# Summing one quad of batches in six float32r passes instead of two float32 products

## The reference

```
h = relu(layernorm(x))
h = relu(adj @ (h @ Wg0 + bg0)); h = relu(adj @ (h @ Wg1 + bg1))     # per batch
for p in 1..4:          # windows of p nodes, an LSTM of p steps over each window
    last = lstm(h[:, windows of p nodes])
    h[:, last node of each window] = last
x = x + h
h = relu(layernorm(x))
V0, V1, V2 = h @ W[0], h @ W[1], h @ W[2]
out = x + diag(adj)*V0 + triu(adj,1) @ V1 + tril(adj,-1) @ V2 + bias
```

## Time and profile before

| what | value |
|---|---|
| median of 3 runs | 393.39 us (393.28 to 394.52) |
| the profiled execution's own time | 394.06 us |
| its span, first to last instruction | 391.6 us |
| PE busy | 386.2 us (99%), 2346 matmuls |
| PEld busy | 341.1 us (87%) |
| DVE busy | 334.4 us (85%), 867 instructions |
| ACT busy | 279.9 us (71%), 556 instructions |
| POOL busy | 64.2 us (16%) |
| TensorE clock granted | 1.000 of full speed, on average over the span |

### The profile page before, as it was taken

The page is one execution under the profiler, slowest core; times in us unless marked ns, Lnnn a source line. Parts: engine busy times, 40 slices in busy tenths (PEclk is TensorE's granted clock), DMA queues, the critical chain, the costliest instruction groups (busy, mean ns, idle before and its releaser), DMA issues.

```text
span 391.6 us, 6502 instructions
## 1 busy us (share of the span) xinstructions
PE 386.2 (99%) x2346; PEld 341.1 (87%) x2346; DVE 334.4 (85%) x867; ACT 279.9 (71%) x556; POOL 64.2 (16%) x67
## 2 busy tenths in 40 slices
PE   8999999999999999999999999999999999999996
PEld 8787899997976889899777889899897788989986
DVE  6669999998988788897998888989798958778895
ACT  4768776876597786777389777777659868667563
POOL 4820200101440003001043000300134000000242
PEclk9999999999999999999999999999999999999999
DMA  6940000005282000122366000030529200000045
GB/s 203 381 191 3 0 0 2 1 2 107 39 140 68 0 28 0 38 98 54 56 109 136 27 2 28 2 134 2 110 27 190 53 0 28 0 28 1 4 77 163
DMA packets 12559, 24.76 MB, mean 63 GB/s; under 512 B 4720, under 2 KB 6000, under 8 KB 11632
## 3 DMA queue, kind: packets, MB, share of 16 engines
q0 software_dynamic: 3600, 10.49, 15.1%
q1 hardware_dynamic: 8928, 13.87, 10.2%
HBM read 16.99 MB, written 4.22 MB: 54 GB/s over the span
## 4 chain that ended last, share of the span: by engine, by line
PE 59%; DVE 5%; DMA 1%; issue 1%; ACT 1%; POOL 1%; DVEq 0%; POOLq 0%
PE PS L612 9%; PE PS L613 9%; PE PS L628 8%; PE PS L659 5%; PE PS L648 5%; PE PS L649 5%; PE PS L708 4%; PE PS L552 2%; PE PS L529 2%; PE PS L562 2%; PE PS L700 2%; PE PS L544 2%; PE PS L701 2%; PE PS L702 2%; DMA X<-bias_row 1%
## 5 line engine op out<-in xcount | busy, mean ns | idle before, releaser
L975 ACT ACTIVATE GT<-PS,BG 128x256 f32<-128x256 f32 (+2 forms) x312 | 158.4, 564 | 16.0 <-PE PS L659 12.5
L612 PE MATMUL PS<-HH,WIH 128*128 128x256 f32 (+2 forms) x312 | 106.2, 341 | 0.3 <-DVE X L1241 0.3
L613 PE MATMUL PS<-HH,WIL 128*128 128x256 f32 (+2 forms) x312 | 102.7, 330 | 0.0
L628 PE MATMUL PS<-HL,WIH 128*128 128x256 f32 (+2 forms) x287 | 94.5, 329 | 0.0
L990 ACT ACTIVATE TC<-CS 128x512 f32<-128x512 f32 (+2 forms) x88 | 44.9, 510 | 45.9 <-DVE CS L1121 33.8
L612 PEld LDWEIGHTS PS<-HH,WIH 128*128 128x128 f32 x312 | 58.7, 188 | 10.0 <-DVE HH L1162 4.2
L430 POOL TENSOR_TENSOR RS<-VE,NHALF 128x4 f32<-128x4 f32 (+2 forms) x18 | 34.0, 1888 | 202.5 <-DVE VE L1057 131.4
L613 PEld LDWEIGHTS PS<-HH,WIL 128*128 128x128 f32 x312 | 58.8, 188 | 4.1 <-issue 1.2
L648 PE MATMUL PS<-SH,WHH 128*128 128x256 f32 (+2 forms) x192 | 59.9, 313 | 0.0
L649 PE MATMUL PS<-SH,WHL 128*128 128x256 f32 (+2 forms) x192 | 59.6, 311 | 0.0
L659 PE MATMUL PS<-SL,WHH 128*128 128x256 f32 (+2 forms) x189 | 59.0, 312 | 0.0
(11 more groups left out here) (107 smaller groups left out, 646.6 us busy)
## 6 DMA issues: line engine op xcount, KB each, us to landing
out_tbd<-X SPq DMA_DIRECT2D x15, 256.0 KB, 2.0
X<-x_tbd SPq DMA_DIRECT2D x3, 1024.0 KB, 11.8
H<-x_dbt SPq DMA_DIRECT2D x3, 1024.0 KB, 5.7
H<-HF POOLq DMA_DIRECT2D x6, 512.0 KB, 4.7
X<-bias_row POOLq DMA_DIRECT2D x6, 512.0 KB, 6.9
H<-means POOLq DMA_DIRECT2D x6, 256.0 KB, 5.1
H<-means POOLq DMA_DIRECT2D x3, 512.0 KB, 5.7
WI<-wih_t SPq DMA_DIRECT2D x1, 1024.0 KB, 5.6
```

Of the source, the lines that this page charges most:

```text
L612: pe.matmul(dst, WIH[:, p - 1, cols], x_high, start=True, stop=False)
L613: pe.matmul(dst, WIL[:, p - 1, cols], x_high, start=False, stop=False)
L628: mm = pe.matmul(dst, WIH[:, p - 1, cols], x_low, start=False, stop=(j == 0))
L975: act.activation(GT[:, s, q, 0:n], bank(s, q)[:, 0:n], ACT.Tanh if q == C else ACT.Sigmoid, bias=BG[:, 4 * (p - 1) + q:4 * (p - 1) + q + 1 ...
```

## The change

Quad 2 of groups 0, 1 and 2 (`PARTED = (2,)`) is summed in another way. ACT rounds V1 and V2 of the quad to float32r in two halves of two batches (256 columns for each side, 512 elements a partition) and puts them into a new tile; this stands in units 10 and 12, between the gates and the tanh. DVE subtracts, also in two halves, and puts the rest into the same tile; this is a `late` piece of units 10 and 12. PE sums the quad in six float32r passes of 512 columns: high parts of adj by high values and low parts of adj by high values for each side, then high parts of adj by low values for each side. The parts of adj's sides (256 columns) are made once, in body 0: the high part by ACT behind unit 18, the low part by DVE behind unit 19.

```
+PARTED = (2,)
+PART = "part"
+HIGH_PART_AT = {10: (2, 0), 12: (2, 1)}
-START_LATE = {4: ((OWN, 0),), 5: ((LOW, 2),), 9: ((LOW, 3),)}
+START_LATE = {4: ((OWN, 0),), 5: ((LOW, 2),), 9: ((LOW, 3),), 10: ((PART, (2, 0)),), 12: ((PART, (2, 1)),)}
-LATE_HIGH_AT = {6: ("wi",), 7: ("wh",), 16: ("wl",)}
-LATE_LOW_AT = {7: ("wi",), 9: ("wh",), 18: ("wl",)}
+LATE_HIGH_AT = {6: ("wi",), 7: ("wh",), 16: ("wl",), 18: ("adj",)}
+LATE_LOW_AT = {7: ("wi",), 9: ("wh",), 18: ("wl",), 19: ("adj",)}
...
+            def parted_sum(g, q, ps):                                   # PE
+                high, low = parts_of(0), parts_of(1)
+                pe.wait_ge(part_high, parted_before(g, q, 1) + 1)
+                for k in range(SIDES):
+                    pe.matmul(ps[:, :], ADJH[:, k, :], high[:, k, :], start=(k == 0), stop=False)
+                    pe.matmul(ps[:, :], ADJL[:, k, :], high[:, k, :], start=False, stop=False)
+                pe.wait_ge(part_low, parted_before(g, q, 1) + 1)
+                for k in range(SIDES):
+                    mm = pe.matmul(ps[:, :], ADJH[:, k, :], low[:, k, :], start=False, stop=(k == SIDES - 1))
+                mm.then_inc(out_mm, 1)
...
+                elif n in PARTED:
+                    parted_sum(g, n, bank(s, F))
...
+                    before = QUADS * g + q - 2                          # ACT, copy_value
+                    if before % QUADS in PARTED and before // QUADS < GROUPS - 1:
+                        act.wait_ge(part_low, parted_before(before // QUADS, before % QUADS, 1) + 1)
...
+            def high_part(g, q, half):                                  # ACT
+                act.wait_ge(value_sb, G * g + q * PACK + (half + 1) * HALF)
...
+                act.activation(halves_of(parts_of(0), half), halves_of(values(q)[:, 1:PARTS, :], half),
+                               ACT.Copy).then_inc(part_high, 1)
...
+                if plan and k in HIGH_PART_AT:
+                    high_part(i - 1, *HIGH_PART_AT[k])
                 act.wait_ge(cell_ready, len(UNITS) * i + k + 1)
...
+            def low_part(g, q, half):                                   # DVE
+                dve.wait_ge(part_high, parted_before(g, q, half) + 1)
+                dve.tensor_tensor(halves_of(parts_of(1), half), halves_of(values(q)[:, 1:PARTS, :], half),
+                                  halves_of(parts_of(0), half).bitcast(F32), ALU.subtract).then_inc(part_low, 1)
```

More of the change, by code:

```diff
@@ L121, with parted_before @@
 PLANS = (None, SECOND) + (GROUPS - 3) * (STEADY,) + (LATE,)
+def parted_before(g, q, half):
+    return 2 * (len(PARTED) * g + PARTED.index(q)) + half
 def present(g, n):
@@ L133, in lows_together @@
     return plan is not None and (k in (9, 15) or plan is SECOND and k == 4)
-LATE_HIGH_AT = {6: ("wi",), 7: ("wh",), 16: ("wl",)}
-LATE_LOW_AT = {7: ("wi",), 9: ("wh",), 18: ("wl",)}
-LATE_ORDER = ("wi", "wh", "wl")
+LATE_HIGH_AT = {6: ("wi",), 7: ("wh",), 16: ("wl",), 18: ("adj",)}
+LATE_LOW_AT = {7: ("wi",), 9: ("wh",), 18: ("wl",), 19: ("adj",)}
+LATE_ORDER = ("wi", "wh", "wl", "adj")
 CELL_EARLY = (1, 2, 15)
@@ L194, in program @@
         ADJ2 = sb("ADJ2", [T, SIDES, T])
+        VP = sb("VP", [T, 2, SIDES * PACK * D], F32R)
+        ADJH = sb("ADJH", [T, SIDES, T], F32R)
+        ADJL = sb("ADJL", [T, SIDES, T], F32R)
         DIAG = sb("DIAG", [T, 1])
@@ L288, in program @@
         value_sb = sem("value_sb")
+        part_high = sem("part_high")
+        part_low = sem("part_low")
         own_ready = sem("own_ready")
@@ L319, in late_parts @@
                 return WH[:, POOL_SKIPS - 1, :], WHH[:, POOL_SKIPS - 1, :], WHL[:, POOL_SKIPS - 1, :]
+            if what == "adj":
+                return ADJ2[:, :, :], ADJH[:, :, :], ADJL[:, :, :]
             return WL1[:, :, :], WLH[:, :, :], WLL[:, :, :]
@@ L324, in values, with parts_of, halves_of @@
             return (WI, WH)[q % 2]
+        def parts_of(n):
+            return VP[:, n, :].rearrange("p (k e) -> p k e", k=SIDES)
+        def halves_of(ap, half):
+            return ap[:, :, half * HALF * D:(half + 1) * HALF * D]
         def quad(q):
@@ L889, in late_split_high @@
                     act.wait_ge(w_hh, 16)
+                elif what == "adj":
+                    act.wait_ge(consts, 6)
                 else:
@@ L923, in copy_value @@
                                scale=RS2[:, n:n + 1]).then_inc(value_sb, 1)
+            def high_part(g, q, half):
+                act.wait_ge(value_sb, G * g + q * PACK + (half + 1) * HALF)
+                if half == 0 and PARTED.index(q):
+                    act.wait_ge(out_mm, QUADS * g + PARTED[PARTED.index(q) - 1] + 1)
+                act.activation(halves_of(parts_of(0), half), halves_of(values(q)[:, 1:PARTS, :], half),
+                               ACT.Copy).then_inc(part_high, 1)
             def last_copy(piece, g):
@@ L1284, in last_step @@
             def last_step(what, g, q, plan):
+                if what == PART:
+                    low_part(g, *q)
+                    return
                 if not present(g, q):
```

## The result

The changed kernel takes 395.11 us (median of 8 runs, 394.81 to 396.11); the kernel before, run beside it, 393.95 us (8 runs, 393.15 to 394.52). The ratio is 1.0033, 95% interval 1.002 to 1.0047: 1.3 us slower by the ratio, between 0.8 and 1.9 us (1.2 us by the two medians). The prediction said 1.5 us slower (394.9 us against a median of 393.39 us). The profiled execution took 394.98 us with a span of 393.0 us, 1.4 us longer than the span before.

The account below looks back on a forecast made before the run. PE, though 99% busy, was taken to wait behind the sum for DVE's rounding of unit 13. Terms 0.45 + 0.45 + 0.3 + 0.3 = 1.5 us slower, from 393.39 to 394.9 us; range 393.0 to 395.9 us.

Parts of the forecast that it names:

- The sum is shorter and gains nothing: PE, quad 2's sum in three bodies: 0.34 us shorter each, 0 gained because PE waits for unit 13's rounding.
- The page's rule for float32: Float32 takes four passes: eight against six, each sum 0.43 us shorter instead of 0.34; worth nothing behind the wait.
- the 0.77 us before the weight load: PEld idle before unit 15's first load, until DVE rounded unit 13's high part; taken as waiting under a busy PE.
- The second subtraction costs 0.45, 0.45, 0.3 us: DVE behind unit 12, no hole: unit 15's first matmul 0.45 us later in bodies 1 and 2, 0.3 in body 3.
- The first subtraction and ACT's copies cost nothing: DVE behind unit 10 and ACT before the tanhs of units 10 and 12: the added work fits existing waits, 0 us.
- The delay is carried to the end: PE behind unit 15: no wait on anything unmoved, so the 0.45 us delay is not taken up again.
- no-change rival: The subtraction's 0.45 us is taken up again later; at most body 0's 0.3 us stays: 393.4 to 393.7 us, chance 0.18.
- Body 0's 0.3 us: DVE's subtraction for adj ahead of unit 20's product delays tanh and stream 0's transposes: 0.3 us, bounds 0 and 0.34.
- faster rival: The saved passes arrive, 0.34 us per sum less body 0's 0.3: 0.7 us faster, 392.7 us, chance 0.10.
- the deciding point: Body 1: whether unit 13's high part comes before the shorter sum ends at 161.28; rounding 0.4 us earlier or subtraction free.

Follow-up runs that it names:

- e2: Changed kernel with all parts still made, but quad 2 summed by the two float32 products: 394.8 us against 393.86 before, ratio 1.003.
- f3: Changed kernel with only two of the six passes (high by high), sum not exact: 394.6 us against 393.6 before, ratio 1.0033.
- f4: Changed kernel with the second half's subtraction behind unit 12 made twice: 396.84 us against 393.6 before, ratio 1.0085.
- e3: Changed kernel with the second half's subtraction moved from behind unit 12 to the middle of unit 13: 394.0 us against 393.86 before, ratio 1.0002.
- e4: As e3, with adj's subtraction also moved, from behind unit 19 to the middle of unit 21: 393.71 us against 393.86 before, ratio 0.9996.
- e1: Kernel before plus only the making of adj's parts in body 0, unused, sums in float32: 393.63 us against 393.86 before, ratio 0.9996.
- g3: As e4, with only the addition of quad 2's sum moved before unit 14's product with the tanh: 392.73 us against 393.41 before, ratio 0.9979.
- g1: As f1, with the addition of quad 2's sum moved before unit 14's product with the tanh: 392.04 us against 393.41 before, ratio 0.9959.
- f1: As e4, with batch 14's value piece right behind quad 2's sum, before unit 15, in bodies 1 and 2: 393.47 us against 393.6 before, ratio 0.9996.
- g2: Kernel before, float32 sums and no parts, with g1's moves of value piece and addition: 392.29 us against 393.41 before, ratio 0.997.

## Why the prediction was right

**The sum is shorter and gains nothing: right.** The step was 0.23 us a pass, 1.38 us in all, and the wait for unit 13 took it up. e2 and f3 show it: with the float32 sum, with six passes and with two, unit 15 starts 2.25 to 2.30 us behind the sum's start. The page's rule for float32 (the Trainium skill, "FP8 and Floating Point Precision", TensorE Precision Notes), weighed in the prediction, had no say here, since no length of the sum mattered. One of the prediction's arguments was weaker than it looked: it called the 0.77 us before the weight load waiting under a busy PE, but PE's own wait was only 0.10 us of it. What carried the forecast was the comparison of the two ends, 161.62 for the sum and 161.66 for the rounding.

**The second subtraction costs 0.45, 0.45, 0.3 us: right.** Sum to next grew by 0.44, 0.45 and 0.29 us. The mechanism stands by three runs: made twice it costs 0.72 us more in each body (f4), moved by one unit it costs nothing (e3), and its use by PE plays no part (e2). For the 0.61 us of a subtraction's turn the prediction pointed at rows that show it for another instruction, the addition L1241; the changed kernel shows it for the subtraction itself (158.82 to 159.43).

**The first subtraction and ACT's copies cost nothing: right by the trace.** The waits that they fill went from 0.78 to 0.17 us on DVE and from 0.84 to 0.32 us on ACT, and from 0.65 us to none shown before the tanh of unit 10 (the prediction said about 0.1 us for both tanhs; by its own sum, 0.84 - 0.55, it was 0.29 us for unit 12). No run took these away by themselves; e3 and e4 keep them and reach the time of before.

**The delay is carried to the end: right.** Behind each body's sum the offset stays to the next body, apart from the DVE wait and the late DMA. The no-change rival would have shown here, and e3 against the changed kernel measures 1.2 us where the three bodies' terms make 1.18 us.

**Body 0's 0.3 us: right at its place, given back elsewhere.** The transposes moved by 0.28 us in the changed kernel, 0.31 us once the 0.03 us is added by which it starts earlier, and by 0.30 us in e1. The prediction said that nothing would take a delay up again; the DVE wait, gone at 187 us, gives 0.33 us back. With it the terms are 0.31 + 0.44 + 0.45 + 0.29 - 0.33 = 1.16 us, against 1.3 us measured (0.8 to 1.9). The predicted 1.5 us lies in the interval too, so the changed kernel's measured time doesn't decide between the two, and the forecast's number would have stood as well with this term missed; the same 0.33 us also closes the sums of e1, g3 and g1 (1.32 + 0.33 = 1.65 us, measured 1.6), and e1 and g3 need it: their intervals exclude 0.30 us slower and 0.33 us faster.

**What the prediction did not see** is that its faster rival couldn't have been reached by making DVE cheaper alone. It put the deciding point at unit 13's state, and gave as one way to the gain that the subtraction takes no time on DVE's path. In e4 it takes none there, and nothing is gained. e4, f1 and g1 show three layers: DVE's cost out of the way gives the time of before; the hole behind the sum filled gives nothing yet, for the bank's addition is late next; with that moved too the kernel is 1.6 us faster, in the traces 1.05 us of it by the two moves (0.33 of this by the addition in body 3), 0.33 by the DVE wait, whose cause is open, and 0.24 by the passes.

## What to carry to other kernels

Before saving passes on the busiest engine, look at what its weight loads wait for right behind them: if the next one waits for another engine's result that ends last, the passes are free already, and the instructions added to that other engine are what is paid. Look for the holes of the other engines (a product that waits for ACT's tanh, an activation that waits for DVE) and put added work into them; the same instruction cost 0.45 us behind unit 12 and nothing half a unit later. And fill a hole only after asking which wait stands behind it.

## What the runs showed of the hardware

- Two pieces of 256 elements in one instruction cost what one row of 512 does: the copy L972 0.621 us on ACT (0.626 for L900), the subtraction L1299 0.687 us on DVE (0.690 for L1170).
- A matmul that was waited for took longer to the next one: 161.72 to 161.94 in the trace of before's body 1, 0.22 us, where 256 columns otherwise follow every 0.11 to 0.12 us. In g1, without a wait, it is 161.71 to 161.82. Behind the sum of bodies 1 to 3 the step is 0.22 or 0.23 us in before and after alike. So a short wait cost about 0.1 us more than its length here. Removing it gave that back: from the sum's start to unit 15's second gate, with the value piece between, it is 2.68 us before and 2.48 us in g2, whose sum is the same, 0.20 us less where the wait was 0.10 us. Why the step is longer no run shows.
- One DMA (the means added to H) came late by enough to cost 0.4 us in two of fourteen traces of much the same program, and 0.15 us in a third; in two more it may have cost 0.08 us.
- DVE waited 0.45 us for its own addition in the four kernels without adj's parts and not in the ten with them, at an instruction that is the same in all, 100 us behind what differs. The cause stays open: no run moved or changed that instruction. Such a step of 0.33 us is as large as most terms of this study, so a run's time should be held against terms only once both traces have been followed matmul by matmul.
